# Moving the first transfers and the product of L0 and L1 at the start of a 1-core kernel

## The reference

```python
x = x + einsum('bct,bcd->bdt', x, L0_weights[tok_16])      # 16 matrices 64x64
x = x + einsum('bct,bcd->bdt', x, L1_weights[tok_16])      # the same token
x = x + einsum('bsi,oi->bso', x, W) + 0.5 * (x @ lora_A[tok_3]) @ lora_B_w.T
x = x + einsum('bsi,boi->bso', x, L3_weight[tok_adapter])
```

## Time and profile before

| | us |
|---|---|
| median of 3 runs | 385.55 (385.03 to 385.63) |
| the profiled execution, own time | 385.22 |
| its span, first to last instruction | 383.4 |
| TensorE busy | 377.7 (98%) |
| VectorE busy | 269.2 (70%) |
| ScalarE busy | 224.4 (59%) |

### The profile page before, as it was taken

One profiled execution on the slowest core, in us unless ns is written; L12 is line 12 of the kernel. 1 busy time (PEld: TensorE's weight loads), 2 busy tenths in 40 slices (PEclk: granted clock), 3 DMA queues, 4 the chain that ended last, 5 costly groups with the idle time before them and its releaser, 6 DMA issues.

```text
span 383.4 us, 7702 instructions
## 1 busy us (share of the span) xinstructions
PE 377.7 (98%) x1760; PEld 315.2 (82%) x1761; DVE 269.2 (70%) x300; ACT 224.4 (59%) x299; POOL 117.8 (31%) x157
## 2 busy tenths in 40 slices
PE   8999999999999999999999999999999999999995
PEld 8888888888888888888888888888888888888784
DVE  3796978856849788537869468963599626989643
ACT  3679558496246476245475465753677546778433
POOL 0000140100000000024766346753268532576500
PEclk9999999999999999999999999999999999999999
DMA  8975904640368384406427315552256522663223
GB/s 271 398 288 175 372 3 150 224 172 5 110 237 287 134 322 136 173 29 218 147 88 233 94 32 191 194 168 59 55 208 206 142 58 58 220 217 119 60 64 85
DMA packets 24187, 61.38 MB, mean 160 GB/s; under 512 B 1906, under 2 KB 2098, under 8 KB 24114
## 3 DMA queue, kind: packets, MB, share of 16 engines
q1 hardware_dynamic: 23792, 60.37, 47.3%
q10 hardware_dynamic: 322, 0.18, 0.2%
HBM read 52.15 MB, written 8.39 MB: 158 GB/s over the span
## 4 chain that ended last, share of the span: by engine, by line
PE 99%; POOL 0%; ACT 0%; issue 0%; ACTq 0%; POOLq 0%
PE ps L1496 45%; PE ps L1364 12%; PE ps L1363 12%; PE ps L1365 12%; PE ps L1390 4%; PE ps L1519 4%; PE ps L1429 3%; PE ps L1584 2%; PE ps L1402 2%; PE ps L1335 1%; PE ps L1343 1%; PE ps L1534 0%; POOL st L452 0%; ACT stage L841 0%; ACTq L840 0%
## 5 line engine op out<-in xcount | busy, mean ns | idle before, releaser
L1496 PE MATMUL ps<-ring,aT 128*128 x752 | 173.4, 389 | 0.0
L1496 PEld LDWEIGHTS ps<-ring,aT 128*128 128x128 f32 x752 | 141.0, 188 | 29.8 <-issue 0.7
L1364 PE MATMUL ps<-ring 128*128 128x512 f32 x208 | 81.0, 389 | 0.0
L1363 PE MATMUL ps<-ring 128*128 128x512 f32 x208 | 81.0, 389 | 0.0
L1365 PE MATMUL ps<-ring 128*128 128x512 f32 x208 | 80.9, 389 | 0.0
L471 POOL TENSOR_TENSOR aT<-xT,aT 128x512 fp32r<-128x512 f32 (+1 forms) x36 | 56.2, 1581 | 45.8 <-ACT aT L754 40.3
L1246 DVE TENSOR_TENSOR ring<-raw,ring 128x1024 f32 (+1 forms) x40 | 64.1, 1659 | 6.2 <-ACT ring L740 6.2
L760 ACT ACTIVATE aT<-ps 64x1024 fp32r<-64x1024 f32 x32 | 32.7, 1021 | 47.6 <-PE ps L1496 47.2
L1274 DVE TENSOR_TENSOR stage<-ps,stage 64x1024 f32<-64x1024 f32 x30 | 36.7, 1222 | 27.5 <-ACT stage L769 26.8
L1263 DVE TENSOR_TENSOR aT<-ps,aT 64x1024 fp32r<-64x1024 f32 x32 | 39.1, 1222 | 21.6 <-ACT aT L760 20.9
L1365 PEld LDWEIGHTS ps<-ring 128*128 128x128 f32 x208 | 39.0, 188 | 8.1
(11 more groups left out here) (94 smaller groups left out, 333.8 us busy)
## 6 DMA issues: line engine op xcount, KB each, us to landing
raw<-w3t SPq DMA_DIRECT2D x40, 512.0 KB, 4.3
ring_f<-xt SPq DMA_DIRECT2D x8, 1024.0 KB, 8.0
raw<-xt SPq DMA_DIRECT2D x8, 1024.0 KB, 5.3
out<-stage SPq DMA_DIRECT2D x30, 256.0 KB, 3.1
ring_f<-wt SPq DMA_DIRECT2D x4, 1024.0 KB, 7.8
xT<-xt SPq DMA_DIRECT2D x3, 1024.0 KB, 11.4
xT<-wt SPq DMA_DIRECT2D x2, 1024.0 KB, 16.2
ring_f<-wt SPq DMA_DIRECT2D x4, 256.0 KB, 5.2
```

The costliest lines, as they stand in the source:

```text
L1363: pe.matmul(dst, hi_of(qw)[:, k, cs], hi_of(qx)[:, k, :], start=start and k == 0, stop=False, skip_group_check=True)
L1364: pe.matmul(dst, hi_of(qw)[:, k, cs], lo_of(qx)[:, k, :], start=False, stop=False, skip_group_check=True)
L1496: last = pe.matmul(acc(i)[:, n, :], x3_split(i, k, start, P), ring[:, bass.ds(off + (part * D + n * 512), 512)], start=(k == 0 and j == 0) ...
```

## The change

On ACT's queue, x tile 0 is issued ahead of `eye`. On SP's queue the two tables `w1_s` and `w0_s` go behind tile 1 of W and x. VectorE no longer adds the three identities at its start: `plus_eye(0)`, `(1)` and `(2)` stand behind `w_lo` of tiles 1, 2 and 3, and the token reads move from tiles 0 and 1 to tiles 2 and 3. TensorE runs 15 warm-up matmuls in place of 20, then P1, and then the product of L0 and L1, with one wait for each of its halves. ScalarE copies `mix_tab` before it scales `b_split` (it was the other way round).

```diff
-WARM, BRIDGE = 20, 6
+WARM, BRIDGE = 15, 6
@@ SP
-            sp.dma_start(w1_s, w1).then_inc(s("w1"), 16)
-            sp.dma_start(w0_s, w0t).then_inc(s("w0"), 16)
             for k in range(HALF):
                 one = slice(k, k + 1)
                 sp.dma_start(raw_of(w_slot(0))[:, one, :], w_block(1, 1)[:, one, :]).then_inc(s(f"w_in0_{k}"), 16)
-                sp.dma_start(raw_of(x_slot(0))[:, one, :], x_block(1, 0)[:, one, :]).then_inc(s(f"x_in0_{k}"), 16)
+
+                if k:
+                    sp.dma_start(raw_of(x_slot(0))[:, one, :], x_block(1, 0)[:, one, :]).then_inc(s(f"x_in0_{k}"), 16)
+                if k == 1:
+                    sp.dma_start(w1_s, w1).then_inc(s("w1"), 16)
+                    sp.dma_start(w0_s, w0t).then_inc(s("w0"), 16)
@@ ACT
+            act.dma_start(raw_of(x_slot(0))[:, 0, :], xt[0, 1, 0]).then_inc(s("x_in0_0"), 16)
             act.dma_start(eye[:, :], eye_c).then_inc(s("eye"), 16)
...
             act.wait_ge(s("mm"), 2)
+            for h in range(2):
+                act.activation(mix_tab[:, 512 * h:512 * (h + 1)], ps_low[:, h, :], ACT.Copy).then_inc(s("mix_tab"), 1)
             act.wait_ge(s("kw"), 16)
             act.activation(b_split[:, :], b_raw, ACT.Copy, scale=0.5).then_inc(s("b_split"), 1)
-            for h in range(2):
-                act.activation(mix_tab[:, 512 * h:512 * (h + 1)], ps_low[:, h, :], ACT.Copy).then_inc(s("mix_tab"), 1)
@@ DVE
+            def plus_eye(n):
+
+                half, quarter = NC_ // 2, NC_ // 4
+                if n == 0:
+                    dve.wait_ge(s("w1"), 16)
+                    v = w1_s.rearrange("p (c n) -> p c n", n=T)
+                    dve.tensor_tensor(v, v, eye[:, P:P + T].unsqueeze(1).to_broadcast([P, half, T]), ALU.add)\
+                       .then_inc(s("w01i"), 1)
+                else:
+                    dve.wait_ge(s("w0"), 16)
...
@@ DVE, the loop over k
                 w_lo(0, raw_of(w_slot(0)), one)
-                if k == 0:
+                if k:
+                    plus_eye(k - 1)
+                if k == 2:
                     dve.wait_ge(s("toks"), 16)
-                if k < 2:
+                if k >= 2:
                     loras += [dve.value_load(toks[0:1, 1, b:b + 1], min_val=0, max_val=NL - 1)
-                              for b in range(CP * k, CP * (k + 1))]
+                              for b in range(CP * (k - 2), CP * (k - 1))]
@@ PE
-            for c in range(NC_ // 2):
-                pe.wait_ge(s("w01i"), 2 if c < NC_ // 4 else 3)
...
+            for c in range(NC_ // 2):
+                if c in (0, NC_ // 4):
+                    pe.wait_ge(s("w01i"), 2 + c // (NC_ // 4))
```

More of the change, by code:

```diff
@@ L867, in _ @@
             dve.wait_ge(s("eye"), 16)
[L868 to L877, removed]
+            def plus_eye(n):
[7 more added lines that the diff above has]
+                    dve.wait_ge(s("w0"), 16)
+                    cs = slice(quarter * (n - 1), quarter * n)
+                    v = w0_s.rearrange("p (c n) -> p c n", n=T)[:, cs]
+                    dve.tensor_tensor(w0_twice[:, cs], v.unsqueeze(2).to_broadcast([P, quarter, 2, T]),
+                                      eye[:, P:P + T].unsqueeze(1).unsqueeze(1).to_broadcast([P, quarter, 2, T]), ALU.add)\
+                       .then_inc(s("w01i"), 1)
             def w_lo(w, src, ks=slice(0, HALF)):
@@ L1432, in _ @@
                             last.then_inc(s("l2"), 1)
+            for c in range(NC_ // 2):
+                if c in (0, NC_ // 4):
+                    pe.wait_ge(s("w01i"), 2 + c // (NC_ // 4))
+                for g in range(2):
+                    rows = slice(g * T, (g + 1) * T)
+                    last = pe.matmul(ps_low[:, g, T * c:T * (c + 1)],
+                                     w0_twice[rows, c, :, :].rearrange("p h n -> p (h n)"),
+                                     w1_s[rows, T * c:T * (c + 1)], start=True, stop=True)
+            last.then_inc(s("mm"), 2)
             product(0, 1, 0, 1, True, True, None, (0, 1))
```

## The result

The changed kernel took 386.97 us in the median of 19 runs (384.93 to 388.26), the one before 385.28 in as many (384.74 to 385.91). The ratio is 1.0033, with a 95% interval of 1.002 to 1.0047. The median lies 0.17 us above the end of the forecast's range and 1.9 us above the forecast; it is the time of the rival "the clock rises late" (387.1). The spread has grown from 1.2 to 3.3 us, and the fastest runs are nearly as fast as those of before (384.93 against 384.74).

A forecast was written before the change was run, and what follows sets the result against it. TensorE's program was taken to bound the kernel. P1's start 5.5 + P1 11.02 + clock 0.2 + product 1.85 = 18.57, against 18.97: 0.4 us earlier, so 385.1 us; range 384.6 to 386.8 for 8 in 10.

The forecast's parts named there:

- the clock rises late: Rival: with TensorE idle from 4.7 to 5.5, up to eleven P1 matmuls run slow; 385.9 to 387.3 us, chance 0.25.
- The start of P1: P1, 48 TensorE matmuls, starts at 5.5 us in place of 7.95, once ScalarE has copied x tile 0; bounds 5.45 to 6.25.
- The product: The 16 matmuls of L0 and L1, now behind P1, take 1.85 us at the upper clock level; bounds 1.76 to 2.03.
- The clock under P1: TensorE's clock rises at 6.05 us as before, so one or two P1 matmuls run slow, costing 0.2 us.
- the warm-up: TensorE's 15 warm-up matmuls end at about 4.7 us, against 5.9; it then idles 0.8 us, removing nothing from the path.
- The bounds of the sum: The next product's first matmul, before at 18.97 us, starts between 18.23 (0.74 earlier) and 18.92 (0.05 earlier).
- VectorE's chain: VectorE's moved instructions under P1 come in time; thinnest at `w_lo` of tile 1, ending at 9.95, with 0.25 to 0.45 us spare.
- ScalarE's swap: Copying `mix_tab` first costs nothing: the copies ran at 21.07 to 22.1 us, and the low-rank product reads them at 24.1.
- From there all as before: Behind the next product's first matmul, TensorE does the same work in the same order, 0.4 us earlier.

## Why the prediction was wrong

**The start of P1: right.** Forecast 5.5, measured 5.59. ScalarE was the last gate, as worked out; its timeline answers the earlier trace rows:

```profile
0.79 0.42 ACTq L562 DMA_DIRECT2D ring_f<-xt  x1
...
3.11 1.28 ACT L660 ACT_TABLE_LOAD   x1 [2.98 <-issue]
4.41 0.52 ACT L660 ACTIVATE ring<-ring_f 128x384 fp32r<-128x384 f32 x1
4.84 0.61 ACT L574 ACTIVATE ring<-ring_f 128x512 fp32r<-128x512 f32 x1
5.71 0.31 ACT L664 ACTIVATE ring<-ring_f 128x128 fp32r<-128x128 f32 x1 [0.27 <-DVE ring_f L1172]
```

Table load at 3.11 (3.1), x copied by 5.45. `eye` came at 5.3 and not at 4.8, 0.27 us after the diagonal's copy could have begun; the three matmuls ahead hid that.

**The product: right.** 1.85 forecast, 20.43 - 18.50 = 1.93 measured.

**The clock under P1: the step that failed.** The forecast took the rise at 6.05 "as before" and so 0.2 us; the clock rose at 9.53, and measured were nine slow matmuls and 12.91 - 11.02 = 1.89 us. Of the miss of 20.43 - 18.57 = 1.86 us this term has 1.69; P1's start has 0.09 and the product 0.08. The mistake stands a paragraph ahead, under the warm-up: "TensorE then idles 0.8 us. That removes nothing from the path by itself, since P1 waits for data." It doesn't by itself, but the rise came late behind it, as the longer matmuls in its place showed. The rival had mechanism, place and price: eleven slow matmuls and +1.6 us at its end, against nine and +1.46 in this trace, eleven or twelve in the second one. It was given a chance of 0.25 because no row showed what a gap does; the kernel's spread of 3.3 us and the two groups of the 15 warm-ups in the kernel before show that it decides most executions, and not all. The range ended at 386.8, inside that rival's 385.9 to 387.3 and not at its end. The bounds of the sum, "with every term at its end", could not show this either: they let the clock cost 0.27 at most, and P1 start at 5.6, where the forecast's own upper bound was 6.25.

The Trainium skill ("TensorE: Matmul & The Clock Gate", Part 1) says that the warm-up is a matter of time and not of a number of matmuls. The runs agree: 15 long matmuls did what 20 did (385.24 and 385.13). The forecast drew from it that five fewer "don't move the rise", though a gap is time without activity.

**VectorE's chain: right in its outcome, wrong in a term.** W tile 2 landed at 3.11 + 7.0 = 10.1, not at 9.0 (issue to landing, us):

```profile
ring_f<-wt SPq DMA_DIRECT2D x1, 256.0 KB, 7.0
```

though as many bytes stood ahead of it. So `w_lo` of tile 1 ended at 11.0 and not at 9.95:

```profile
8.38 0.69 DVE L899 TENSOR_TENSOR ring<-ring_f,ring 128x512 fp32r<-128x512 f32 x1 [1.30 <-ACT ring L574]
10.12 0.29 DVE L1172 TENSOR_TENSOR ring_f<-ring_f,eye 128x128 f32<-128x128 f32 x1 [1.04 <-DMA ring_f<-wt]
10.32 0.68 DVE L892 TENSOR_TENSOR ring<-ring_f,ring 128x512 fp32r<-128x512 f32 x1
```

The slow matmuls hid it here. With 20 warm-ups the tile's diagonal ran at 9.2 and P1 had no stall; with x on SP's queue the same kind of lateness, one tile ahead, did stall P1. The lateness isn't the change's doing alone. With the same transfers, the diagonal that waits for this tile ran at 9.2 in the second trace of the changed kernel, and at 8.7 with 25 warm-ups: the landing differs by more than a microsecond between executions, and the forecast's 9.0 lies among them. Why it does wasn't tried.

**ScalarE's swap: right.** The copies of `mix_tab` ran at 21.11, the low-rank product started at 26.01 and didn't wait.

**"From there all as before": wrong by what was gained.** The forecast carried the 0.4 us to the end because TensorE had no wait in 383 us. No wait doesn't mean slack: at 54.8 there was none, and what arrives 0.2 to 0.6 us sooner may wait there for 0.2 to 0.4. With 20 warm-ups, so that there is no gap, the change is worth 0.17 us by the medians (385.13 against 385.30), which can't be told from nothing (0.9964 to 1.0005). The forecast's sum had said why: the product lost its cover, which the run with the product moved alone puts at 1.7 us.

## What to carry to other kernels

Warm-up matmuls are there to keep TensorE at work until its first real ones can start; when these are moved ahead or the warm-up is cut, look at the time between the last of one and the first of the other, and not at their number. In the kernel before they also stood in the product's way for 0.5 us, and to take five of them out still lost by the median: four executions gained 0.7 us and eight lost 3. Work that runs while the first tiles land is nearly free there and costs its full length behind them, so the gain of an earlier start has to be set against it first. An engine that never waits has been met just in time at some places: read the distance to the releaser at those, ahead of carrying a gain to the end.

## What the runs showed of the hardware

- A gap of 0.7 us behind 15 warm-up matmuls went with a rise of TensorE's clock at 9.53 and 10.71 us in the two traces of the changed kernel, and cost 1.7 us in the median. With the same cut in the kernel before, four of twelve executions showed no loss; the one that was traced had a gap of 0.5 us and its rise at 5.49.
- With TensorE busy from its first matmul up to the rise, the rise still moved from execution to execution: 4.86 to 7.56 us in eleven traces. With 20 warm-ups P1 was at the upper level from its first matmuls (rise at 5.81), and only after four in the trace with `low_sum(1)` ahead (7.56), by the number of matmuls in the same 2 us, eleven in the first and eight in the second:

```profile
5.50:7.50 2.00, 2.00 (x11) 1.00 0.90 305
5.50:7.50 2.00, 2.00 (x8) 1.00 0.98 323
```

- At the lower level a warm-up matmul of 192 columns took as long as one of 256 (4.58 and 4.61 us for 20), and one of 352 took 0.29 us (15 in 4.60 us). Between 192 and 256 columns the moving columns aren't what sets the pace.
- The granted clock in the windows read 1.00 at both paces. In each trace the record of it begins where the pace changes, and the stretch ahead of it, at 1.2 GHz, has no record.
